# Token weights of a mixture-of-experts layer: laid out expert by expert in HBM, and multiplied in by two engines

## What is computed

```python
topk_idx, tw = _route(x, router_w, bias)              # 2 of 4 groups, then 4 of 16 experts; weights sum to 2.5
combine = (one_hot(topk_idx, E) * tw[..., None]).sum(1)   # (1024 tokens, 16 experts)
h = jnp.einsum('td,edf->etf', x, gate_w)
u = jnp.einsum('td,edf->etf', x, up_w)
y = jnp.einsum('etf,efd->etd', silu(h) * u, down_w)
routed = jnp.einsum('etd,te->td', y, combine)
sh = silu(x @ sh_gate_w) * (x @ sh_up_w) @ sh_down_w
```

## Time and profile before

| | us |
|---|---|
| median of 3 runs | 237.54 |
| lowest, highest | 235.93, 238.69 |
| the profiled execution | 237.24 |
| its span, first to last instruction | 235.3 |
| TensorE, matmuls busy | 200.3 |
| POOL busy | 127.7 |
| DVE busy | 124.4 |
| ScalarE busy | 100.8 |

### The profile page before, as it was taken

The page is one execution under the profiler, slowest core; times in us unless marked ns, Lnnn a source line. Parts: engine busy times, 40 slices in busy tenths (PEclk is TensorE's granted clock), DMA queues, the critical chain, the costliest instruction groups (busy, mean ns, idle before and its releaser), DMA issues.

```text
span 235.3 us, 4499 instructions
## 1 busy us (share of the span) xinstructions
PE 200.3 (85%) x1597; PEld 136.1 (58%) x1597; DVE 124.4 (53%) x271; ACT 100.8 (43%) x241; POOL 127.7 (54%) x207
## 2 busy tenths in 40 slices
PE   6688899989999999999998259987999789497952
PEld 5456566666678777777857115645676356264611
DVE  4824578575698877888796014597322213023211
ACT  2364888978577644557754011321222213122200
POOL 5366355983514899787684158648620260264560
PEclk9979999999999999999999857997999958979998
DMA  5850000000510840000001453743302504555421
GB/s 122 314 150 0 3 6 4 3 3 0 149 36 0 249 110 0 1 3 0 0 4 19 93 104 82 119 116 96 91 9 33 126 22 68 110 103 136 108 57 45
DMA packets 28983, 15.83 MB, mean 67 GB/s; under 512 B 1681, under 2 KB 28706, under 8 KB 28834
## 3 DMA queue, kind: packets, MB, share of 16 engines
q1 hardware_dynamic: 28962, 15.56, 26.9%
HBM read 14.96 MB, written 0.59 MB: 66 GB/s over the span
## 4 chain that ended last, share of the span: by engine, by line
PE 45%; DMA 34%; ACT 5%; DVE 5%; issue 4%; SPq 3%; POOL 2%; POOLq 1%; DVEq 0%; ACTq 0%
DMA wkv_sb<-w_rows 30%; PE bank L1599 7%; PE wide L1570 6%; PE bank L1547 3%; PE bank L1671 3%; PE bank L1555 3%; PE bank L1584 3%; PE bank L1540 2%; PE wide L1629 2%; PE wide L1631 2%; PE wide L1630 2%; DMA wq_sb<-in_L_xattn_w_q_dram 2%; DMA w_rows<-w_rows_sb 2%; PE bank L1597 1%; PE bank L1455 1%
## 5 line engine op out<-in xcount | busy, mean ns | idle before, releaser
L832 ACT ACTIVATE kbd<-wide 128x512 f32<-128x512 f32 x36 | 21.5, 598 | 78.0 <-PE wide L1631 39.6
L1629 PE MATMUL wide<-x3hi,gu_lo 128*128 128x512 f32 x72 | 41.5, 577 | 2.9 <-POOL gu_lo L553 2.5
L563 POOL TENSOR_TENSOR vbd<-s,wkv_sb 128x512 f32<-128x512 f32 x16 | 20.4, 1277 | 36.2 <-DMA wkv_sb<-w_rows 28.6
L1671 PE MATMUL bank<-vbd,wq_sb 128*128 128x512 f32 x32 | 21.6, 776 | 13.4 <-POOL vbd L563 13.2
L563 POOL TENSOR_TENSOR vbd<-p,wkv_sb 128x512 f32<-128x512 f32 x16 | 20.3, 1274 | 21.4 <-DMA wkv_sb<-w_rows 15.4
L1259 DVE TENSOR_TENSOR p<-kbd,wide 128x512 f32<-128x512 f32 x18 | 12.3, 685 | 36.0 <-PE bank L1671 20.4
L1630 PE MATMUL wide<-x3lo,gu_hi 128*128 128x512 f32 x72 | 30.1, 418 | 0.0
L1631 PE MATMUL wide<-x3hi,gu_hi 128*128 128x512 f32 x72 | 30.0, 417 | 0.0
L1259 DVE TENSOR_TENSOR s<-kbd,wide 128x512 f32<-128x512 f32 x18 | 12.3, 684 | 29.7 <-PE bank L1671 17.6
L1629 PEld LDWEIGHTS wide<-x3hi,gu_lo 128*128 128x128 f32 x72 | 14.6, 203 | 13.4 <-issue 7.6
L1671 PE MATMUL bank<-vbd,wqT 128*128 128x512 f32 x32 | 17.3, 624 | 4.0 <-POOL vbd L563 3.9
(11 more groups left out here) (157 smaller groups left out, 404.6 us busy)
## 6 DMA issues: line engine op xcount, KB each, us to landing
wkv_sb<-w_rows SPq DMA_DIRECT2D x32, 256.0 KB, 8.1
wkv_sb<-in_L_xattn_w_kv_dram SPq DMA_DIRECT2D x1, 1024.0 KB, 6.9
v<-in_L_ffn_gate_w_dram SPq DMA_DIRECT2D x4, 256.0 KB, 4.4
v<-in_L_ffn_up_w_dram SPq DMA_DIRECT2D x4, 256.0 KB, 5.8
wq_sb<-in_L_xattn_w_q_dram SPq DMA_DIRECT2D x1, 512.0 KB, 4.5
wout_sb<-in_L_xattn_w_out_dram SPq DMA_DIRECT2D x1, 512.0 KB, 6.1
wq_sb<-in_L_ffn_down_w_dram SPq DMA_DIRECT2D x1, 512.0 KB, 3.8
wqT<-in_L_ffn_down_w_dram SPq DMA_DIRECT2D x1, 512.0 KB, 5.5
```

The lines of the kernel that those rows point to most:

```text
L563: pool.tensor_tensor(aw[k % 3], act[k % 4], spread[:, r % SPREAD, :, :].rearrange("p t q -> p (t q)"), ALU.mult).then_inc(awp_s, 1)
L832: sc.activation(sil[:, k % 2, :], bank[up_bank(k)], ACT.Silu).then_inc(sil_s, 1)
L1629: pe.matmul(dst, lo, x3hi[:, cols], start=True, stop=False)
L1671: pe.matmul((FOLD, PV)[c], dn_of(n), rhs, start=(n == 0), stop=(n == NE - 1)).then_inc(y_s, 1)
```

## The change

`w_rows` is laid out chunk, expert, tile, so that the four rows of an expert lie together: a spread load reads one piece of 2 KB for each partition where it read four of 512 B. `store_rows` writes a chunk in four transfers, one for each tile, since the tiles' rows lie apart now. `BY_VECTOR` holds the odd units: DVE weighs those, POOL the even ones. And the lists of calls of all engines are in another order.

```diff
--- before.py
+++ after.py
@@ -181,7 +181,7 @@
         nmean = sb("nmean", [P, 3, NT, 1])
         w_rows_sb = sb("w_rows_sb", [P, NCH, P])
         y_sb = sb("y_sb", [P, CHUNK])
-        w_rows = nc.dram_tensor("w_rows", (NCH, P // 2, P), F32, kind="Internal").ap()
+        w_rows = nc.dram_tensor("w_rows", (NCH, E, TPC, P), F32, kind="Internal").ap()
 
         spread = wkv_sb[:, :].rearrange("p (s t q) -> p s t q", s=SPREAD, t=TPC)
@@ -309,7 +309,7 @@
 
         NK = NE * NCH
         ONE_PAIR = 4
-        BY_VECTOR = ()
+        BY_VECTOR = range(1, NK, 2)
 
         def routed(k):
@@ -379,19 +379,19 @@
                 c, e = k // NE, k % NE - NSH
                 r = loads_before(k)
                 if e == 0:
-                    sp.wait_ge(rows_st, 16 * (c + 1))
+                    sp.wait_ge(rows_st, 16 * TPC * (c + 1))
                 if r < SPREAD:
                     sp.wait_ge(f_copied, unit_no[("kv", NPAIR - 1)] + 1)
                 else:
                     used = [n for n in range(k) if routed(n)][r - SPREAD]
                     sp.wait_ge(*weighted(used))
                 sp.dma_start(spread[:, r % SPREAD, :, :],
-                             w_rows[c].rearrange("(t e) q -> e t q", e=E)[e].partition_broadcast(P)
-                             ).then_inc(sp_l[r % SPREAD], 16)
+                             w_rows[c, e].partition_broadcast(P)).then_inc(sp_l[r % SPREAD], 16)
 
             def store_rows(c):
                 sp.wait_ge(rows_s, c + 1)
-                sp.dma_start(w_rows[c], w_rows_sb[0:TPC * E, c, :]).then_inc(rows_st, 16)
+                for t in range(TPC):
+                    sp.dma_start(w_rows[c, :, t, :], w_rows_sb[E * t:E * (t + 1), c, :]).then_inc(rows_st, 16)
 
             def store_out(c):
                 sp.wait_ge(fin_s, c + 1)
...
@@ DVE, last block of its row
             multiply(4)
             multiply(5)
+            biased_scores(1)
+            group_scores(1)
+            weigh(3)
             multiply(6)
...
```

More of the change, by code:

```diff
@@ L623, in _ @@
             norm_apply(2, 1)
-            split_hi(4)
-            norm_p2(4)
+            norm_p2(3)
+            split_hi(2)
+            norm_scale(2, 2, 1.0, LN_EPS)
+            norm_apply(2, 2)
+            norm_p2(4)
+            norm_apply(1, 7)
+            split_hi(3)
+            split_lo(2)
+            norm_scale(2, 3, 1.0, LN_EPS)
+            norm_apply(2, 3)
+            norm_p2(5)
+            split_lo(3)
+            split_hi(4)
+            norm_scale(2, 4, 1.0, LN_EPS)
+            norm_apply(2, 4)
+            norm_p2(6)
+            norm_scale(2, 5, 1.0, LN_EPS)
+            norm_apply(2, 5)
+            norm_p2(7)
+            split_lo(4)
             split_hi(5)
             split_hi(6)
[L628 to L631, removed]
+            norm_scale(2, 6, 1.0, LN_EPS)
+            split_lo(5)
+            norm_apply(2, 6)
             split_hi(7)
[L633 to L650, removed]
             norm_scale(2, 7, 1.0, LN_EPS)
             norm_apply(2, 7)
+            split_lo(6)
+            split_hi(8)
+            split_hi(9)
+            split_lo(7)
+            split_lo(8)
+            split_hi(10)
             split_hi(11)
-            split_lo(8)
             split_lo(9)
@@ L851, in _ @@
             scale_qk(1)
+            copy_fold(("kv", 0))
             copy_qkT(1)
+            exp1(0)
             copy_xnT(2)
@@ L975, in _ @@
             exp_logits(7)
+            copy_rows(0)
             silu(3)
-            copy_rows(0)
             silu(4)
@@ L992, in _ @@
             silu(18)
+            copy_rows(1)
             silu(19)
             silu(20)
-            copy_rows(1)
             silu(21)
+            copy_y(0)
             silu(22)
             silu(23)
-            copy_y(0)
             silu(24)
@@ L1830, in _ @@
             output2(4, 0)
+            output2(4, 1)
             transpose_xn(1, 7, T1[:, 0:P])
[L1832 removed]
             transpose_p2(5, 0)
+            transpose_xn(2, 3, T1[:, P:2 * P])
             scores2(7)
[L1835 removed]
             transpose_p2(5, 1)
+            output2(5, 0)
             logits(3)
[L1838 removed]
+            transpose_xn(2, 4, T1[:, P:2 * P])
             output2(5, 1)
             transpose_p2(6, 0)
+            up(0)
+            logits(4)
+            transpose_p2(6, 1)
+            output2(6, 0)
             gate(0)
[L1842 to L1846 removed]
+            transpose_xn(2, 5, T1[:, P:2 * P])
             output2(6, 1)
             transpose_p2(7, 0)
+            gate(1)
+            logits(5)
+            transpose_p2(7, 1)
             gate(2)
[L1850 to L1851 removed]
+            output2(7, 0)
+            output2(7, 1)
             up(1)
[L1853 to L1864 removed]
+            transpose_xn(2, 6, T1[:, P:2 * P])
+            gate(3)
+            logits(6)
+            gate(4)
+            transpose_xn(2, 7, T1[:, P:2 * P])
+            down(0)
+            logits(7)
+            up(2)
+            transpose_rows(0)
             down(1)
             up(3)
[L1867 removed]
             up(4)
@@ L1949, in _ @@
             gate(32)
+            down(27)
             up(31)
             gate(33)
+            down(28)
+            gate(34)
             up(32)
-            down(27)
-            down(28)
             down(29)
             up(33)
+            up(34)
             down(30)
-            gate(34)
+            down(31)
             gate(35)
-            up(34)
-            down(31)
             up(35)
```

497 lines of the change are left out of this document (233 added, 264 removed).

## The result

The changed kernel takes **208.88 us** in the median of 4 runs (206.64 to 212.91), the one before 237.44 on the same chip (235.93 to 238.69): a ratio of 0.873, with a 95% interval of 0.863 to 0.883. Two of the four executions (209.85 and 212.91 us) ran in a slower state of the chip, and the ratio is taken from the other two, 207.3 us in the mean. The forecast was 213 us, range 206 to 229. The profiled execution took 206.64 us, its span is 204.9.

A forecast was written before the change was run, and what follows sets the result against it. Late spread loads of token weights starve TensorE, losing 32 us of a 106.4 us stage. Start 124.1 plus 74 of work plus 8 of losses gives 206.1; 4.8 of tail and 1.9 more give 213 us, range 206 to 229.

The forecast's parts named there:

- Landing: Spread loads of token weights: landing falls from 8.1 to 4 us, from 3.3 worked out plus some queueing.
- all ask for the same few addresses: Reason given for slow spread loads: 128 copies of the same 2 KB, the first of a burst at 43 GB/s.
- first rival: Spread loads land no sooner, as 2 KB may lie in one place limited to 43 GB/s: 228 us, chance 0.27.
- Order and stores at the first chunk: Chunk 0's routing, four stores and first loads: TensorE waits 1.0 us, then 1.5 for downs 2 to 4; 2.5 lost.
- Border: Between chunks: earlier row copy and add_y(0) free the store and load 24; 1.5 us of loss kept.
- Lock between DVE and POOL: Odd weighings on DVE, blocked by POOL's weighings: a fifth of a 1 us delay in 16 cases, 3 us.
- Rest: Loss of 1 us for what remains of the stage; the undisturbed stretch 163.9 to 182.7 had lost 0.4.
- TensorE's work: Stage from 124.1 us without waits at 2.4 GHz: 63 products, 34 downs and transposes, 74 us, ending at 198.1.
- Slower rival: Odd weighings on DVE wait for late loads with multiplies behind them, if loads stay slow: 242 us, chance 0.06.
- since TensorE then can't work ahead: Step in the slower case: of 22 us DVE waits for loads, 14 more fall on the path.
- what was to show it right: Landings near 4 us, first over 100 GB/s; gap under 3; no POOL wait near 9; load 24 behind weigh(20); some DVE weighings near 1.9.
- sign of being wrong: Spread loads still landing at 7.5 us, or TensorE waiting over 5 us in all for DVE's weighings.

The follow-up runs named there:

- e: Changed kernel with each load's piece split into four of 512 B lying 1 KB apart, four stores: 210.62 us, ratio 0.881.
- f: Changed kernel with four pieces of 512 B lying 8.5 KB apart (padding of one 512 B row), four stores: 210.48 us, ratio 0.890.
- run a: Changed kernel with the row layout and single store of before, all new orders and the split of weighings kept: 223.54 us, ratio 0.948.
- f_pieces_8k: Changed kernel with four pieces of 512 B lying 8 KB apart as in the old layout, but four stores: 226.33 us, ratio 0.950.
- run h: Changed kernel with DVE's group_scores(1) moved behind multiply(7), so weigh(3) no longer stands behind it: 207.35 us, ratio 0.867.

## Why the prediction was right, point by point

The forecast was 213 us, measured 208.88. The profiled execution, whose rows are compared here, took 206.64, so against the rows the forecast misses by 2.2 us more. The prediction had the last `down` end at 206.1; it ends at 200.16. TensorE's own work from 122.73 on is 76.28 us, to 199.0 where the forecast had 198.1: 0.9 too little. The losses were put at 8 and are 1.15. Together 5.9 us. The mechanism was right, late spread loads that starve TensorE by way of the weighings; the sizes of the losses were too large, and two reasons were wrong:

- **Landing, 4 us taken, 3.3 measured.** That is the value that the prediction had worked out before it added 0.7 for queueing. The size was right and its reason was wrong: "all ask for the same few addresses" is not what slows a load. Runs e and f read the same 512 bytes 128 times as before and land in 3.5 and 3.8 us; the 8-KB distance does it. The neighbours in the earlier trace rows ran together at 179 GB/s, and I read from that that four neighbours are quick, which happened to hold for either cause: the 3.3 us came out right by luck. The first rival ("2 KB may lie in one place") is shut out.
- **Order and stores at the first chunk, 2.5 us lost forecast, 1.14 measured.** Weights ready at 122.4 in the forecast; `combine` ended at 121.69 + 0.38 = 122.07. The last store landed at 126.3 in the forecast; the first load left at 126.09. The first weighing could begin at 130.3 in the forecast and began at 129.34: the landing again. Downs 3 and 4 were to wait 1.5 us for loads in a row; the one wait is 1.14 and not for a load but for DVE, held up by POOL.
- **Border, 1.5 us kept, 0 measured.** The 29.30 us to 163.9 and the 36.26 after them have no gap. The step put this down to the order. Either half of the change brings it: the border's orders alone gave 13.8 us of the stage, and nothing beside the new layout, which alone gave 26.4 of the 29.0.
- **Lock between DVE and POOL, 3 us, 1.14 measured (the same gap).** I counted collisions of weighings with weighings. Of DVE's 16, one shows more than 0.7 us:

```profile
L1251 DVE TENSOR_TENSOR vbd<-p,wkv_sb x8: 676/684/694, 132.5 to 197.7; 128x512 f32<-128x512 f32 x8
L1251 DVE TENSOR_TENSOR vbd<-s,wkv_sb x8: 683/692/1112, 137.3 to 194.6; 128x512 f32<-128x512 f32 x8
```

  What collides is the routing of chunk 1. And it is a matter of phase: in run f with 8.5 KB, DVE's list is that of the changed kernel, but POOL's instructions start later against DVE's (`weigh(6)` 15.0 us behind the start of the stage where the changed kernel has 13.4, DVE's `weigh(5)` at 14.6 in both), and the same place reads

```profile
139.23 1.76 DVE L1251 TENSOR_TENSOR vbd<-p,wkv_sb 128x512 f32<-128x512 f32 x1
140.91 1.29 DVE L1156 TENSOR_TENSOR cmp_b<-r_g 128x64 f32<-128x64 f32 x1
142.13 0.76 DVE L1157 TENSOR_TENSOR cmp_a<-r_g 128x64 f32<-128x64 f32 x1
142.92 0.65 DVE L1159 TENSOR_TENSOR cmp_a<-cmp_a,lower 128x64 f32<-128x64 f32 x1
```

  where the changed kernel has 0.68, 0.21, 0.21 and 0.22, and TensorE waits 2.5 us for the multiply behind. The changed kernel's second run has 0.72 us for its one gap. So the term lay between 0.7 and 2.5 us, without the clock that a long gap costs; 3 us was above all of them, and it was met at another instruction than I named. The rule cited from the Trainium skill ("SBUF — State Buffer", Who interferes with whom) covers these, which all have two SBUF inputs (a DVE instruction with two of them contends with a GpSimd one that reads SBUF); and the 36 multiplies, with one input in PSUM, all last 673 to 689 ns in both runs.
- **Rest, 1 us, 0 measured.**
- **TensorE's work.** 74 us from 124.1 was the estimate; from 122.73 it took 76.28, two products more than in the kernel before. The earlier start makes up for 1.4 of the 2.3.
- **First rival (loads no sooner), 228 us.** Built as run a: 223.5 us, or 225.1 by its ratio of 0.948, so its terms were too dear by 3 to 4.5 us. One of them, 9.8 us for the first gap, stands in no row: the rows give 9.1, and 9.8 is the round of a slot.
- **Slower rival (DVE stands in front of late loads), 242 us.** The condition was met in run a, landing 8.0 us, and DVE waited 23.0 us where the prediction had 22. But 14 us of it were to reach TensorE, and 5.2 did in run a. The step that failed there is "since TensorE then can't work ahead": `up(k)` asks for `multiply(k-2)`, and mostly had it. In `f_pieces_8k` DVE waited 27.2 us, and TensorE 5.1 for DVE and 4.2 for ScalarE, of which at least the 3.6 shown above stood behind DVE; that kernel took 226.3 us. Neither comes near 242.

Of what was to show it right, all came but one: no weighing on DVE came near 1.9 us, the longest took 1.11. Neither sign of being wrong came.

## What to carry to other kernels

A transfer that is slower than its size explains is to be asked about the distance between its pieces, before their number: pad one row and look at the landing and the DMA share of the first one in the burst. Where two repairs act on one late chain (quicker loads; earlier issue with the split), their gains do not add: here 26.4 and 14.8 us make 29.0, so each is to be priced with the other already made. And where two engines lock each other out, what it costs depends on the moment at which they meet, so moving the instruction that is seen to wait may only move the wait, as it did in run h.

## What the runs showed of the hardware that was not expected

Four pieces of 512 B, read by 128 partitions, 2.0 us behind the issue of the first load: 8 KB apart 43 GB/s, 8.5 KB apart 173, 1 KB apart 285. One piece of 2 KB gives no more at that moment, in the changed kernel run beside the last two:

```profile
128.87:129.87 1.00, 1.00 (x6) 0.82 (x5) 0.97 (x3) 0.52 (x1) 0.22 (x1) 1.00 0.94 285
```

though its first profiled execution moved 328 there. A padding of one row of 512 B, which takes the landing from 8.0 to 3.8 us, gives nearly all of the landing that merging the pieces gives (3.3).

The granted clock in the first 30 us lay between 0.77 and 1.00 from one profiled execution to the next, and with one order of instructions it shifted the start of the stage by up to 3.2 us, more than several of the differences that the experiments were made for.
